# The negated maximum as three bfloat16 words, split by GpSimd, and new instruction orders in an attention and expert kernel

## What is computed

```python
x = x + attention(layernorm(x), ctx, pos)      # 32 heads of 8, 64 keys per sequence, rotary positions on q and k
x = x + experts(layernorm(x))                  # 8 experts, the best 2 of each token, hidden width 176

logits = einsum('bqhd,bkhd->bhqk', q, k) / sqrt(8)
w = softmax(logits); attn = einsum('bhqk,bkhd->bqhd', w, v)
```

## Time and profile before

| | us |
|---|---|
| median of 3 runs (529.56 to 529.92) | 529.66 |
| the profiled execution | 529.24 |
| its span | 527.3 |
| TensorE busy (share of the span) | 474.1 (90%) |
| VectorE busy | 405.5 (77%) |
| GpSimd busy | 366.0 (69%) |
| ScalarE busy | 351.6 (67%) |
| L1369, the product that adds the maxima | 34.3 |

### The profile page before, as it was taken

The page is one execution under the profiler, slowest core; times in us unless marked ns, Lnnn a source line. Parts: engine busy times, 40 slices in busy tenths (PEclk is TensorE's granted clock), DMA queues, the critical chain, the costliest instruction groups (busy, mean ns, idle before and its releaser), DMA issues.

```text
span 527.3 us, 21533 instructions
## 1 busy us (share of the span) xinstructions
PE 474.1 (90%) x7701; PEld 365.8 (69%) x7701; DVE 405.5 (77%) x1199; ACT 351.6 (67%) x929; POOL 366.0 (69%) x634
## 2 busy tenths in 40 slices
PE   3676899999999999999999999889899999899890
PEld 2563566676676766767666665559799999889780
DVE  7376689899898999999989898767655556776672
ACT  3473677877778777777777777667466666566550
POOL 4442758888888888888888887356666557675471
PEclk9787999999999999999999999899899999999895
DMA  6920101121121212212111110143654446877844
GB/s 192 235 71 7 30 20 54 40 74 43 60 66 49 94 52 70 65 48 67 40 61 56 50 35 25 44 120 96 195 158 132 127 127 202 251 236 240 303 146 159
DMA packets 43225, 54.55 MB, mean 103 GB/s; under 512 B 6727, under 2 KB 36849, under 8 KB 43122
## 3 DMA queue, kind: packets, MB, share of 16 engines
q1 hardware_dynamic: 36066, 35.79, 24.5%
q0 software_dynamic: 6480, 16.85, 8.9%
q10 hardware_dynamic: 576, 0.53, 0.3%
HBM read 29.60 MB, written 23.94 MB: 102 GB/s over the span
## 4 chain that ended last, share of the span: by engine, by line
PE 69%; DVE 12%; DMA 6%; issue 6%; SPq 2%; ACT 2%; POOL 2%; POOLq 0%; DVEq 0%; ACTq 0%
PE logit_banks L1551 9%; PE bank L1401 6%; PE logit_banks L1570 6%; PE logit_banks L1361 6%; PE logit_banks L1342 5%; PE bank L1388 5%; PE qkv_banks L1310 5%; PE logit_banks L1369 5%; PE bank L1394 4%; PE qkv_banks L1321 3%; DVE negmax L757 3%; PE qkv_banks L1301 3%; DMA y_in<-result_rows 3%; PE bank L1331 3%; PE bank L1539 2%
## 5 line engine op out<-in xcount | busy, mean ns | idle before, releaser
L691 POOL DMA_INDIRECT result_rows<-blocks_io,blk_dest x71 | 72.5, 1021 | 53.3 <-ACT blocks_io L1245 23.8
L657 POOL DMA_INDIRECT routed_rows<-xs,slots x64 | 65.7, 1026 | 16.7 <-issue 16.7
L757 DVE TENSOR_REDUCE negmax<-logit_banks 128x16 f32<-128x1024 f32 x64 | 75.0, 1212 | 2.3 <-PE logit_banks L1342 2.3
L1137 ACT ACTIVATE late<-logit_banks 128x1024 f32<-128x1024 f32 x64 | 62.0, 1021 | 14.4 <-PE logit_banks L1369 14.4
L664 POOL TENSOR_TENSOR ropes<-rope_a,ropes 128x512 f32<-128x512 f32 x32 | 41.2, 1288 | 29.5 <-DVE ropes L744 29.5
L1022 DVE TENSOR_TENSOR gated<-xn,logit_banks 128x176 f32<-128x176 f32 x71 | 23.8, 335 | 46.8 <-ACT xn L1251 45.8
L764 DVE RECIPROCAL rden<-bank 128x256 f32<-128x256 f32 x32 | 55.8, 1745 | 0.8 <-PE bank L1394 0.8
L648 POOL TENSOR_TENSOR mid<-mid,mask 128x512 f32<-128x512 f32 x44 | 44.7, 1035 | 11.8 <-ACT mid L1118 11.7
L1551 PE MATMUL logit_banks<-w_hi,x_hi 128*128 x142 | 47.0, 331 | 0.0
L1551 PE MATMUL logit_banks<-w_hi,x_lo 128*128 x142 | 46.4, 327 | 0.0
L1251 ACT ACTIVATE xn<-logit_banks 128x176 f32<-128x176 f32 x71 | 22.5, 316 | 35.7 <-PE logit_banks L1551 35.7
(11 more groups left out here) (219 smaller groups left out, 1378.8 us busy)
## 6 DMA issues: line engine op xcount, KB each, us to landing
blocks_io<-routed_rows SPq DMA_DIRECT2D x71, 129.0 KB, 2.4
y_in<-result_rows SPq DMA_DIRECT2D x16, 512.0 KB, 4.6
x_sb<-in_x_dram SPq DMA_DIRECT2D x32, 128.0 KB, 2.1
out_dram<-o_sb SPq DMA_DIRECT2D x16, 256.0 KB, 3.8
ctx_sb<-in_ctx_dram SPq DMA_DIRECT2D x32, 64.0 KB, 2.3
blocks_io<-in_L_ffn_W_dram SPq DMA_DIRECT2D x4, 512.0 KB, 6.8
mid<-mT SPq DMA_DIRECT2D x128, 4.0 KB
routed_rows<-pad_row SPq DMA_DIRECT2D x11, 129.0 KB, 2.9
```

Source lines behind the costliest of these rows:

```text
L657: nc.gpsimd.indirect_dma_start(routed[:, :], bass.IndirectOffsetOnAxis(ap=slots[:, t.slot(TR), k:k + 1], axis=0), xs[:, t.slot(TR), k, :], ...
L691: nc.gpsimd.indirect_dma_start(results[:, :], bass.IndirectOffsetOnAxis(ap=blk_dest[:, b.slot(RB):b.slot(RB) + 1], axis=0), y_sb[:, b.slot ...
L757: V.tensor_reduce(negmax[:, t.par, 16 * half:16 * half + 16], ps_s[:, 1024 * half:1024 * half + 1024].rearrange("p (h k) -> p h k", k=N), ...
L1137: S.activation(pT[:, 1024 * half:1024 * half + 1024], ps_s[:, 1024 * half:1024 * half + 1024], ACT.Exp, scale=SCALE).then_inc(exp_done, 1)
```

## The change

The negated maximum gets three words for each head, `negmax` 128 x 96. VectorE writes the first; GpSimd, in a new stage `split_max` with two subtractions of 128 x 32, writes what the leading 16 bits of the first leave, and what the leading 16 bits of the second leave. All 96 rows are transposed, copied and sent, and the product that adds them is one in bfloat16 with three contraction rows, which reads the leading halves of the float32 words. `ps_rank` moves to the bank of the attention output, so `rank` no longer waits for the readers of the query bank; those waits go to `transpose_max`, and `attend` and `residual` get a wait for the rank products. On four engines the order within a period changes. Left out of the diff below: the memset of the row of ones that is no longer needed, and the sizes of the tiles.

```diff
 # GpSimd
+            def split_max(t):
+                pool.wait_ge(max_done, t.times(2, 2))
+                nc.gpsimd.tensor_tensor(maxima(t.par, 1), maxima(t.par, 0), leading(t.par, 0), ALU.subtract)\
+                    .then_inc(parts_step, 1)
+                pool.wait_ge(parts_step, t.n + 1)
+                nc.gpsimd.tensor_tensor(maxima(t.par, 2), maxima(t.par, 1), leading(t.par, 1), ALU.subtract)\
+                    .then_inc(parts_done, 1)
...
                 do(rotate, t.plus(2))
                 if t.plus(4).within(T) or t.plus(-2).within(T):
                     pair(t)
+                do(split_max, t.plus(1))
                 do(normalise_x, t.plus(4))
                 do(mask_keys, t.plus(2))
 # SyncE
-                    sp.dma_start(ms[32 * r:32 * r + 1, :].rearrange("a (g n) -> a g n", n=P),
-                                 mT[8 * r:8 * r + 8, t.par, :]).then_inc(ms_in, 16)
+                    sp.dma_start(ms[32 * r:32 * r + 3, :].rearrange("s (g n) -> s g n", n=P),
+                                 mT[24 * r:24 * r + 24, t.par, :]).then_inc(ms_in, 16)
 # VectorE
             def residual(t):
                 dve.wait_ge(out_done, t.n + 1)
+                wait_past(dve, rank_done, t.n)
...
                 do(peak, t.plus(1))
+                do(invert_sums, t.plus(-1))
+                do(normalise_attn, t.plus(-1))
                 do(best_scores, t.plus(-2))
                 do(best_experts, t.plus(-2))
                 do(mark_choices, t.plus(-2))
                 do(join_choices, t.plus(-2))
-                do(invert_sums, t.plus(-1))
-                do(normalise_attn, t.plus(-1))
                 do(place_tokens, t.plus(-2))
 # ScalarE
                 do(copy_kqT, t.plus(2))
+                do(copy_v, t.plus(1))
                 do(copy_mT, t.plus(1))
-                do(normalise_x1, t.plus(-2))
                 do(exponential, t, 0)
                 do(exponential, t, 1)
-                do(copy_v, t.plus(1))
                 do(copy_xT, t.plus(4))
+                do(normalise_x1, t.plus(-2))
                 do(set_shares, t.plus(-2))
 # TensorE
             def transpose_max(t):
-                pe.wait_ge(max_done, t.times(2, 2))
+                pe.wait_ge(parts_done, t.n + 1)
                 wait_past(pe, mT_sb, t.n)
+                pe.wait_ge(rope_done, upto(t.n + 2))
+                pe.wait_ge(gate_x_done, upto(t.n + 2))
...
-                    row = slice(32 * r, 32 * r + 1)
+                    row = slice(32 * r, 32 * r + 3)
                     for c in range(KC):
-                        ins = M.matmul(banks[r][64 * c:64 * c + 64, :], ones_row[row, :],
-                                       ms[row, :].rearrange("p (g c k) -> p g c k", c=KC, k=N)[:, :, c, :],
+                        ins = M.matmul(banks[r][64 * c:64 * c + 64, :], ones_bf[row, 0:N],
+                                       ms[row, :].bitcast(BF16).rearrange("p (g c k w) -> p g c k w", c=KC, k=N, w=2)[
+                                           :, :, c, :, 1],
...
                 pe.wait_ge(top_done, t.n + 1)
                 wait_past(pe, chosen_done, t.n)
-                pe.wait_ge(mT_sb, upto(t.n + 4))
-                pe.wait_ge(rope_done, upto(t.n + 5))
-                pe.wait_ge(gate_x_done, upto(t.n + 5))
...
                 do(transpose_kq, t.plus(2))
+                do(project_v, t.plus(1))
+                do(shifted_logits, t)
                 do(transpose_max, t.plus(1))
-                do(shifted_logits, t)
+                do(project_k, t.plus(3))
+                do(transpose_x, t.plus(4))
+                do(project_out, t.plus(-1))
                 do(rank, t.plus(-2))
-                do(project_k, t.plus(3))
-                do(project_v, t.plus(1))
-                do(project_out, t.plus(-1))
                 do(project_q, t.plus(3))
-                do(transpose_x, t.plus(4))
```

More of the change, by code:

```diff
@@ L123, in xattn_ffn_kernel @@
                                                                        ps_nd, ps_tr]
-        ps_q, ps_a, ps_rank = ps_qkv[:, 0:D], ps_qkv[:, D:D + E], ps_qkv[:, D + E:D + 2 * E]
-        last_ranks = ps_nd[:, D + E:D + 4 * E]
+        ps_q, ps_a = ps_qkv[:, 0:D], ps_qkv[:, D:D + E]
+        ps_rank, last_ranks, ps_half = ps_nd[:, D + E:D + 2 * E], ps_nd[:, D + E:D + 4 * E], ps_nd[:, D + 4 * E:D + 5 * E]
         ps_cnt = last_ranks[:, 2 * E:3 * E]
-        ps_mT = ps_qkv[0:HEADS, D + 2 * E:D + 2 * E + P]
-        ps_half = ps_qkv[:, D + 2 * E + P:D + 3 * E + P]
+        ps_mT = ps_qkv[0:3 * HEADS, D + 2 * E:D + 2 * E + P]
         ps_k, ps_v = ps_qkv[:, 512:768], ps_qkv[:, 768:1024]
@@ L148, in xattn_ffn_kernel @@
         rope_a = sb("rope_a", [P, 512])
-        negmax = sb("negmax", [P, 2, HEADS])
-        mT = sb("mT", [HEADS, 2, P])
-        ones_row = sb("ones_row", [P, N])
+        negmax = sb("negmax", [P, 2, 3 * HEADS])
+        mT = sb("mT", [3 * HEADS, 2, P])
         rden = sb("rden", [P, D])
@@ L268, in xattn_ffn_kernel, with maxima, leading @@
         rope_b, rot = ropes[:, 0], ropes[:, 1]
+        def maxima(par, part, r=slice(0, RG)):
+            return negmax[:, par].rearrange("p (r s h) -> p r s h", r=RG, s=3)[:, r, part]
+        def leading(par, part):
+            return negmax[:, par].bitcast(BF16).rearrange("p (r s h w) -> p r s h w", r=RG, s=3, w=2)[:, :, part, :, 1]
         x_hi = sb("x_hi", [P, 2, D], FR)
@@ L302, in xattn_ffn_kernel @@
         kqT_done, kqT_sb, km_done, qm_done = (sem(s) for s in ("kqT_done", "kqT_sb", "km_done", "qm_done"))
+        parts_done, parts_step = sem("parts_done"), sem("parts_step")
         s_done, max_done, mT_done, mT_sb, ms_in, st_done, exp_done, pv_done = (
@@ L331, in xattn_ffn_kernel @@
         o_stored = [sem(f"o_stored{n}") for n in range(4)]
-        N_POOL_CONST, N_DVE_CONST, N_W = 10, 11, 2
+        N_POOL_CONST, N_DVE_CONST, N_W = 10, 10, 2
         NW12 = E * KC
@@ L755, in peak @@
                 dve.wait_ge(s_done, t.n + 1)
+                wait_past(dve, mT_done, t.n - 1)
                 for half in range(2):
-                    V.tensor_reduce(negmax[:, t.par, 16 * half:16 * half + 16],
-                                    ps_s[:, 1024 * half:1024 * half + 1024].rearrange("p (h k) -> p h k", k=N),
+                    V.tensor_reduce(maxima(t.par, 0, slice(2 * half, 2 * half + 2)),
+                                    ps_s[:, 1024 * half:1024 * half + 1024].rearrange("p (r h k) -> p r h k", r=2, k=N),
                                     AX_X, ALU.max, negate=True).then_inc(max_done, 1)
@@ L841, in step @@
                 dve.wait_ge(dve_step, steps[0])
-            V.memset(ones_row[:], 1.0).then_inc(dve_const, 1)
             V.memset(vst, 0.0).then_inc(dve_const, 1)
@@ L1299, in project_k @@
                 wait_past(pe, rope_done, t.n)
-                wait_past(pe, v_sb, t.n - 2)
+                wait_past(pe, v_sb, t.n - 1)
                 M.matmul(ps_k, xT[:, t.slot(TR), D:D + P], wk_p[:], start=True, stop=True)
@@ L1306, in project_q @@
                 wait_past(pe, gate_x_done, t.n)
-                wait_past(pe, rank_read, t.n - 4)
                 wait_past(pe, mT_sb, t.n - 1)
@@ L1382, in attend @@
                     wait_past(pe, gate_done, t.n)
+                    wait_past(pe, rank_read, t.n - 1)
                 probs = pT.rearrange("p (r b h k) -> p r b h k", r=RG, b=2, k=N)
```

## The result

| | before | after |
|---|---|---|
| median, same chip | 529.79 us (529.56 to 529.94) | 539.81 us (537.60 to 541.09) |
| the profiled execution | 529.24 | 537.6 |
| its span | 527.3 | 535.7 |
| mean granted TensorE clock | 0.962 | 0.978 |

What follows compares the result with a forecast made beforehand. TensorE was taken to set the period, GpSimd and VectorE close behind. Terms +17.8, +2, -0.5, -2.2 and -3.5 gave +13.6 on 529.24, 542.8; median 543 us, range 528 to 549.

Steps and rivals of the forecast that it cites:

- Mechanism: Attention half: the router meets GpSimd's mask, `chosen` is held, then `rank`, `place`, residual, rope and rotation follow; forecast chance 0.71.
- One sign: VectorE's `onehot`, like `chosen`, was to take up to 1 us, ending with a mask operation.
- The 25 periods: Periods with the whole chain lengthen from 9.36 to 10.07 us each, +17.8 us in all.
- lower case: If only `chosen` is held by the second mask operation, it ends 0.2 us earlier; takes 5 us off the time.
- The block tables: VectorE's expert tables in five periods, formerly hidden before the residual, cost up to 0.4 us each, +2 us.
- The split: Two dependent 128 x 32 subtractions on GpSimd add 0.58 us a period, bounds 0.41 to 1.20.
- The product: TensorE's product adding the maxima falls from 0.99 to 0.27 us in bfloat16, bounds 0.25 to 0.99.
- The ends: First two periods without router -2.2 us; last two periods -0.5; reciprocal first at the end -3.5.
- Nothing held: Rival: mask holds no router operation, `chosen` ends at 5.4, period 9.49 us, time 527 us; chance 0.17.
- A product that is not shorter: Rival: reading two bytes of every four gains nothing, `rank` starts later, 548 to 555 us; chance 0.06.
- The clock: Rival: TensorE's new idle gaps put a third of each period at half clock, about 578 us; chance 0.04.
- The gain as meant: Rival: period of 8.9 us or less, TensorE again the bound, 511 us; chance 0.02.

## Why the prediction was right

The forecast, slower because the router falls into the mask, at 543 us, came out at 539.81. On the profiled executions +13.6 was forecast and +8.4 measured; between the medians it is +10.0. Part of the nearness is luck: the ordinary periods were put 9.8 us too high, and the tables, the beginning and the end 2.2, 0.9 and 1.2 us too low. By terms:

**Mechanism: right.** `chosen` ends with the second mask operation, `place` waits for `rank`, the residual and the next rope follow, and the rotation waits for them. The reduction in place of `chosen` shows it by taking the hold away (9.68 to 9.32). One sign failed: `onehot` was to be held too and takes 0.16.

**The 25 periods, +17.8 and +2 for the tables: +12.5.** I took the ordinary period as 10.07; it is 9.68. I let each mask operation let one instruction through and `chosen` start only after that, to end at 6.41 after the rotation; it is queued already while the second mask operation runs and ends with it, at 143.48 - 137.38 = 6.10. `place` starts at 6.40, not 6.69, and from there to the next rotation pass 3.28 us, not 3.38, which together is 0.39 a period. The prediction named an earlier release of `chosen` as its lower case, with 0.2 a period.

**The block tables, +2: about +4.2.** Six periods (9.78, 10.31, 10.98, 11.01, 10.02, 10.14) exceed 9.67 by 4.2 together; in the kernel before the same six exceed 9.34 by 0.3. The rows show one reason that I had not costed: tiny table operations on VectorE are long too.

```profile
213.92 0.65 DVE L988 TENSOR_SCALAR full_skip<-full_cnt 128x8 f32<-128x8 f32 x1
224.84 0.73 DVE L991 TENSOR_TENSOR full_jump<-full_past,full_skip 128x8 f32<-128x8 f32 x1
```

In the kernel before each takes 0.17. Both stand beside GpSimd's second scatter and end 0.12 and 0.14 us after it (213.48 + 0.97 and 224.47 + 0.96). What held them was not tried.

**The split, 0.58: 0.52.** From `bias` to `xn` pass 0.69 us with it (140.20 to 140.89) and 0.17 without. **The product, 0.27: 0.39,** between the bounds; it hides, since TensorE waits anyway.

**The ends, -2.2 and -4.0: -1.27 and -2.82, and for the second my reason is not shown.** Two residuals of VectorE near the end of the attention half, before and after:

```profile
340.84 0.42 DVE L777 TENSOR_TENSOR xres<-bank,xres 128x256 f32<-128x256 f32 x1 [0.69 <-PE bank L1401]
356.20 0.43 DVE L777 TENSOR_TENSOR xres<-bank,xres 128x256 f32<-128x256 f32 x1
```

```profile
348.89 0.42 DVE L796 TENSOR_TENSOR xres<-bank,xres 128x256 f32<-128x256 f32 x1
367.44 0.41 DVE L796 TENSOR_TENSOR xres<-bank,xres 128x256 f32<-128x256 f32 x1
```

Counted from the end of the 25 periods (304.64 and 315.86), the first of the two, of the third tile from the end, comes 3.2 us earlier in the changed kernel (33.03 for 36.20): up to there a gain near the forecast one is seen. The residual of the last tile comes no earlier (51.58 and 51.56), nor does the last `slots` (58.26 and 58.45, the points where the windows below begin): the gain is lost before the last tile. The first expert block's product, which TensorE starts ahead of that tile's residual, comes no earlier either (46.67 and 46.56); shortly before it TensorE waits 3.20 us for VectorE (`x_lo`), 1.76 before. So the attention half as a whole gave back nothing at its end. Windows of the rest, before and after (length, busy us of PE, PEld, DVE, ACT, POOL, granted clock, DMA share, GB/s):

```profile
363.09:527.33 164.24, 141.33 (x996) 133.84 (x994) 98.45 (x317) 92.89 (x270) 99.26 (x210) 0.94 0.61 187
```

```profile
374.12:535.73 161.61, 138.59 (x996) 131.72 (x994) 98.21 (x317) 92.47 (x270) 101.53 (x210) 0.96 0.62 190
```

The same instructions take 2.6 us less, at a granted clock of 0.96 instead of 0.94. The clock alone does not explain it: in the run with the bfloat16 product alone the same stretch has 0.96 too.

```profile
351.89:516.05 164.16, 139.57 (x996) 132.14 (x995) 98.25 (x318) 92.61 (x270) 99.31 (x210) 0.96 0.62 187
```

In the other experiments it lasts 159.4 to 162.3 us, and 159.8 with VectorE's old order in the changed kernel, so the place of the reciprocal does not set it. What does stays open. Without these 2.6 us the profiled execution would stand at +11.0.

**The rivals.** Nothing held: out, by `chosen`'s 0.89. A product that is not shorter: out. The clock: TensorE's new waits (0.37 and 0.56) brought no stretch at half clock: the granted clock is 1.00 from 69 to 350 us. The gain as meant needed a split that costs GpSimd nothing; with no split and the old orders that period, 8.93, is there, though with GpSimd and not TensorE as the bound.

## What to carry to other kernels

Try the cheap part of a change alone: here the bfloat16 product in the old orders gains 2%, and the words and the orders that came with it turn that into a loss of 1.9%. When an order is changed on one engine, lay the moved instructions beside what the other engines run at that moment: a 0.2 us instruction that lands beside a 2 us one can take four times as long, and it matters if something waits for it: `chosen` at 0.89 cost 0.36 us a period, `seen` at 1.01, in another order, nothing. Orders on two engines belong together: VectorE's old order under TensorE's new one is worse (9.91 us a period) than both as changed (9.68) or both with the router early (9.34).

## What the runs showed of the hardware

A VectorE operation with two SBUF inputs that starts beside GpSimd's two-input mask operation is held until the mask operation running ends (`chosen` 0.89, `gap` 0.67, `seen` 1.01), one VectorE operation passes between two consecutive mask operations (`onehot` 0.16), and a reduction over a single SBUF input is not held (`chosen` in that form, 0.17). That says nothing of every one-input operation: `full_skip`, with one tensor input, took 0.65 beside a scatter. The Trainium skill, SBUF — State Buffer, section "Who interferes with whom", has a VectorE instruction with two SBUF inputs contend with a GpSimd instruction that reads SBUF, under an exclusive lock; the run with the one-input mask doesn't agree, `place` taking 0.16 and `seen` 0.21 inside such an instruction, though `gap` beside `xn` (0.28, to its end) does. Unexpected as well: GpSimd's copy of 128 x 512 with one tensor input took 1.48 us, its product with two 1.02; and two bytes of every four as a bfloat16 operand cost the product 0.39 us, not the quarter of 0.99.
